# Four token mixers and a low-rank feed-forward network on one NeuronCore: where the network's first rows and fixed weights are loaded

## What is computed

```
x = x + L1_attn(_layernorm(x))             # Mamba2 mixer, chunked scan
x = x + L1_xattn(_layernorm(x), ctx, ctx)  # 8-head attention on the context
x = x + L1_ffn(_layernorm(x))              # low-rank experts:
  probs = softmax(x @ Wr + br); w, idx = top_k(probs, 2)
  h = x @ W1 + b1;  t1 = x @ A1 (8 experts, rank 16)
  a_e = gelu(h + 2 * t1_e @ B1_e)          # the two chosen experts
  mix = sum_e w_e * a_e;  t2_e = (w_e * a_e) @ A2_e
  out = mix @ W2 + sum(w) * b2 + 2 * sum_e t2_e @ B2_e
```

## Time and profile before

| | us |
|---|---|
| median of 3 runs | 3318.68 |
| lowest and highest run | 3313.62, 3318.94 |
| the profiled execution | 3309.98 |
| its span in the trace | 3308.3 |
| mean granted TensorE clock | 0.964 of full |
| TensorE, VectorE, ScalarE, POOL busy | 92%, 71%, 48%, 24% |

### The profile page before, as it was taken

One profiled execution on the slowest core, in us unless ns is written; L12 is line 12 of the kernel. 1 busy time (PEld: TensorE's weight loads), 2 busy tenths in 40 slices (PEclk: granted clock), 3 DMA queues, 4 the chain that ended last, 5 costly groups with the idle time before them and its releaser, 6 DMA issues. The chain is left out here.

```text
span 3308.3 us, 61051 instructions
## 1 busy us (share of the span) xinstructions
PE 3039.4 (92%) x22689; PEld 2437.3 (74%) x22689; DVE 2338.8 (71%) x4405; ACT 1597.3 (48%) x3656; POOL 803.8 (24%) x968
## 2 busy tenths in 40 slices
PE   7999999997998799999999859898999979999999
PEld 5666666664887688888888746666667668888888
DVE  5666666664765588888888666778786777777776
ACT  3333333342221455555555426566565756555555
POOL 1221122121454111111111153241423012222222
PEclk9999999998999899999999979899999989999999
DMA  6324233221121577777777621212110032222222
GB/s 261 128 71 175 108 128 110 108 102 39 29 57 34 198 239 238 247 250 243 243 243 240 236 82 65 71 39 72 58 59 20 8 126 89 74 74 77 74 74 71
DMA packets 144825, 401.85 MB, mean 121 GB/s; under 512 B 39056, under 2 KB 47760, under 8 KB 131680
## 3 DMA queue, kind: packets, MB, share of 16 engines
q1 hardware_dynamic: 106176, 323.30, 28.5%
q0 software_dynamic: 18976, 50.45, 5.2%
q10 hardware_dynamic: 19456, 25.18, 2.2%
HBM read 344.09 MB, written 54.76 MB: 121 GB/s over the span
## 5 line engine op out<-in xcount | busy, mean ns | idle before, releaser
L1465 POOL DMA_INDIRECT xg<-normed_rows,idx x128 | 124.8, 975 | 668.4 <-PE psum L1547 591.9
L2661 POOL TENSOR_TENSOR mixf<-act 128x256 f32<-128x256 f32 x128 | 143.5, 1121 | 470.5 <-DVE act L2942 470.5
L174 POOL TENSOR_SCALAR ve<-mv 128x1 f32<-128x1 f32 x112 | 36.7, 328 | 842.3 <-DVE mv L774 590.5
L1562 PE MATMUL psum<-xT_hi,wgu_hi 128*128 128x192 f32 (+1 forms) x1536 | 228.5, 271 | 4.2 <-ACT aT_lo L1529 4.2
L1562 PE MATMUL psum<-xT_lo,wgu_hi 128*128 128x192 f32 (+1 forms) x1536 | 223.3, 268 | 0.0
L1562 PE MATMUL psum<-xT_hi,wgu_lo 128*128 128x192 f32 (+1 forms) x1536 | 222.6, 267 | 0.0
L1601 DVE TENSOR_TENSOR wgu_lo<-wgu,wgu_hi 128x1408 fp32r<-128x1408 f32 x128 | 202.6, 1623 | 22.0 <-ACT wgu_hi L1489 22.0
L1562 PEld LDWEIGHTS psum<-xT_hi,wgu_hi 128*128 128x128 f32 (+1 forms) x1536 | 190.6, 182 | 28.8 <-ACT wgu_hi L1489 21.2
L1502 ACT ACTIVATE eth<-psum 128x192 f32<-128x192 f32 (+1 forms) x192 | 63.2, 329 | 298.1 <-PE psum L1562 295.2
L2019 ACT ACTIVATE scratch<-psum,smin 128x512 f32<-128x512 f32 x256 | 173.7, 686 | 58.3 <-DVE smin L2411 55.3
L2411 DVE TENSOR_REDUCE smin<-psum 128x2 f32<-128x1024 f32 x128 | 155.5, 1218 | 64.7 <-PE psum L2173 40.8
(11 more groups left out here) (436 smaller groups left out, 8592.9 us busy)
## 6 DMA issues: line engine op xcount, KB each, us to landing
wgu<-in_w_gu_dram SPq DMA_DIRECT2D x64, 1408.0 KB, 6.0
w_slot<-w_split SPq DMA_DIRECT2D x21, 2048.0 KB
wd<-in_w_d_dram SPq DMA_DIRECT2D x64, 512.0 KB, 8.7
w_raw<-in_w_dram SPq DMA_DIRECT2D x128, 256.0 KB, 2.6
expert_out<-yo ACTq DMA_DIRECT2D x64, 256.0 KB, 5.2
w_slot<-w_split SPq DMA_DIRECT2D x28, 512.0 KB
wd<-in_w_d_dram SPq DMA_DIRECT2D x64, 192.0 KB, 9.0
w_split<-w_slot SPq DMA_DIRECT2D x4, 2048.0 KB
```

The lines of the kernel that those rows point to most:

```text
L1465: pool.indirect_dma_start(out=xg[b][0:w, t, :], out_offset=None, in_=rows, in_offset=bass.IndirectOffsetOnAxis(ap=idx[b][0:w, t:t + 1], ax ...
L1562: ins = pe.matmul(bank(2 + m)[0:w, gu * CAP:(gu + 1) * CAP], wgu2[b][wp][:, gu, kc, m0:m0 + w], xT2[b][xp][:, kc, :], start=(i == 0 and kc ...
L2661: pool.tensor_tensor(mixf[:, g % LAG, :], act2[:, g % LAG, 0, :], act2[:, g % LAG, 1, :], ALU.add).then_inc(sy["f_mix"], 1)
```

## The change

In the last pair of `mixers`, SyncE issues three loads ahead of the load of the last context: the rows of sequence 0 from `mixed` into `xn[0]`, the first 1024 columns of `w_fixed` into `xn[1]`, and the last 32 (the router's) into a new small tile `router_raw`. They wait for the residuals of the sequences before and for the store of sequence 0. VectorE does the statistics of these rows in steps 12 and 13 of the last score loop and the norm in steps 18 and 19, in place, and POOL the reciprocal root. `xn[0]`, `xn[1]` and `router_raw` live on into `lora_ffn`, where the first two are `xin` and `xo`. There SyncE begins with the expanding pieces, then the small constants, and waits for the stores of `mixed` after these; at the end of `mixers` it waits for the two new loads alone. ScalarE and VectorE split the fixed weights in two instructions each, for 1024 and 32 columns.

```diff
@@ mixers, SyncE, in `for p in range(npair)`
+                if p + 1 == npair:
+                    sp.wait_ge(sy["resid_ready"], NT * first)
+                    sp.wait_ge(sy["mixed_out0"], 16)
+                    sp.dma_start(xn[0][:], dr["mixed"][0]).then_inc(sy["f_x_in"], 16)
+                    sp.dma_start(xn[1][:].rearrange("p t d -> p (t d)"), dr["w_fixed"][:, 0:NT * D]
+                                 ).then_inc(sy["f_fixed_in"], 16)
+                    sp.dma_start(router_raw[:], dr["w_fixed"][:, NT * D:NT * D + KC * LE]
+                                 ).then_inc(sy["f_fixed_in"], 16)
                 sp.wait_ge(sy["cx_lo_ready"], first + 1)
                 load_cx(second)
...
-            for b in range(2):
-                sp.wait_ge(sy[f"mixed_out{b}"], 16 * npair)
+            sp.wait_ge(sy["f_x_in"], 16)
+            sp.wait_ge(sy["f_fixed_in"], 32)
@@ mixers, POOL, end of a pair
+                else:
+                    norm(0, 2 * nseq)
@@ mixers, VectorE
+            def next_apply(j):
+                dve.wait_ge(sy["rstd_ready"], NT * 2 * nseq + j + 1)
+                dve.tensor_scalar(xn[0][:, j, :], xn[0][:, j, :], mv[0][:, j, 0:1], rstd[0][:, j:j + 1],
+                                  ALU.subtract, ALU.mult).then_inc(sy["normed_ready"], 1)
...
                     if i in (PAIRS + 3, HP + 3):
                         attended(first + i // PAIRS - 1, 1)
+                    if not more and i == 12:
+                        dve.wait_ge(sy["f_x_in"], 16)
+                    if not more and i in (12, 13):
+                        stats(0, i - 12, xn[0])
+                    if not more and i in (18, 19):
+                        next_apply(i - 18)
@@ lora_ffn, tiles and SyncE
-        xin, xo = sb("xin", [P, NT, D]), sb("xo", [P, NT, D])
+        xin, xo = rows
...
-        fixed_raw = act2[:].rearrange("p l k t -> p (l k t)")[:, 0:2 * D + KC * LE]
+        fixed_raw = [(slice(0, NT * D), xo[:].rearrange("p t d -> p (t d)")),
+                     (slice(NT * D, NT * D + KC * LE), router_raw[:])]
...
-            load_x(0)
-            for dst, src in ((fixed_raw, "w_fixed"), (br[:], "br_col"), (bias1[:], "bias1"),
-                             (bias2_bc[:], "bias2_bc")):
-                sp.dma_start(dst, dr[src]).then_inc(sy["f_fixed_in"], 16)
             for f in range(RAW):
                 load_up(f)
+            for dst, src in ((br[:], "br_col"), (bias1[:], "bias1"), (bias2_bc[:], "bias2_bc")):
+                sp.dma_start(dst, dr[src]).then_inc(sy["f_fixed_in"], 16)
+            for b in range(2):
+                sp.wait_ge(sy[f"mixed_out{b}"], 16 * nseq // 2)
...
+                        else:
+                            sp.wait_ge(sy["f_fixed_lo"], 1)
                         sp.dma_start(xo[:], dr["mixed"][s]).then_inc(sy["f_xo_in"], 16)
@@ lora_ffn, POOL, ScalarE, VectorE
-            rstd_pool(pool, sy, norms, mv, ve, rstd, const["minus_half"])
...
-            act.wait_ge(sy["f_fixed_in"], 16 * 4)
-            act.activation(fixed2[0][:], fixed_raw, ACT.Copy).then_inc(sy["f_fixed_hi"], 1)
+            act.wait_ge(sy["f_fixed_in"], 16 * 2)
+            for cols, raw in fixed_raw:
+                ins = act.activation(fixed2[0][:, cols], raw, ACT.Copy)
+            ins.then_inc(sy["f_fixed_hi"], 1)
...
+            act.wait_ge(sy["f_fixed_in"], 16 * 5)
             logits_copy(0)
...
-            stats(0)
-            layernorm_apply(dve, sy, norms, xin, xin, mv, rstd)
             dve.wait_ge(sy["f_fixed_hi"], 1)
-            dve.tensor_tensor(fixed2[1][:], fixed_raw, fixed2[0][:].bitcast(F32), ALU.subtract
-                              ).then_inc(sy["f_fixed_lo"], 1)
+            for cols, raw in fixed_raw:
+                ins = dve.tensor_tensor(fixed2[1][:, cols], raw, fixed2[0][:, cols].bitcast(F32), ALU.subtract)
+            ins.then_inc(sy["f_fixed_lo"], 1)
```

More of the change, by code:

```diff
@@ L1671, with mixer_weights @@
 SCALING = 2.0
-def mixer_weights(nc, ctx, dr):
+def mixer_weights(nc, ctx, dr, rows):
     shapes = {"w_in": [P, KC, D + XBC + MH], "small": [P, 64], "w_mo": [P, KC, D]}
@@ L1683, in mixer_weights, with mixers @@
     for s in range(4):
-        tiles[f"xn{s}"] = ctx.enter_context(nc.sbuf_tensor(f"xn3{s}", [P, NT, D], F32))
+        tiles[f"xn{s}"] = (rows[s] if s < len(rows) else
+                           ctx.enter_context(nc.sbuf_tensor(f"xn3{s}", [P, NT, D], F32)))
         loads.append((tiles[f"xn{s}"][:], dr["mid"][s]))
     return tiles, loads
-def mixers(nc, sy, const, dr, tiles, nseq=NSEQ):
+def mixers(nc, sy, const, dr, tiles, router_raw, nseq=NSEQ):
     with ExitStack() as ctx:
@@ L2533, with lora_ffn @@
 UPW = D + 2 * P
-def lora_ffn(nc, sy, const, dr, norms, nseq=NSEQ):
+def lora_ffn(nc, sy, const, dr, rows, router_raw, norms, nseq=NSEQ):
     with ExitStack() as ctx:
@@ L3076, in program @@
         dr["mixed"] = nc.dram_tensor("mixed", [NSEQ, P, NT, D], F32).ap()
[L3077 to L3080, removed]
+        with ExitStack() as carried:
+            rows = [carried.enter_context(nc.sbuf_tensor(f"xn3{b}", [P, NT, D], F32)) for b in range(2)]
+            router_raw = carried.enter_context(nc.sbuf_tensor("router_raw", [P, KC * LE], F32))
+            with ExitStack() as held:
+                tiles, loads = mixer_weights(nc, held, dr, rows)
+                if 2 in phases:
+                    phase2(nc, sy, const, dr, loads)
+                if 3 in phases:
+                    mixers(nc, sy, const, dr, tiles, router_raw, nseq)
             if 3 in phases:
-                mixers(nc, sy, const, dr, tiles, nseq)
-        if 3 in phases:
-            lora_ffn(nc, sy, const, dr, 2 * nseq, nseq)
+                lora_ffn(nc, sy, const, dr, rows, router_raw, 2 * nseq, nseq)
 def cols_layout(w):
```

## The result

| | before | after |
|---|---|---|
| median of 7 runs, us | 3318.68 | 3306.13 |
| lowest and highest | 3313.62, 3322.54 | 3303.8, 3311.08 |
| profiled execution, span | 3309.98, 3308.3 | 3304.07, 3302.3 |
| ratio after to before | | 0.9971, interval 0.9962 to 0.9980 |

The changed kernel is faster, by 6.6 to 12.6 us at this interval. The medians lie 12.5 us apart, the two profiled executions 6.0, and the forecast was 7.1. On another chip the same two kernels gave 0.9981 (0.9972 to 0.9990), 6.5 us between the medians. Both intervals hold the 6.7 us that the traces show at the place of the change.

The account below looks back on a forecast made before the run. At the boundary no engine was the bound, but a chain of single steps without work beside it. Boundary 8.0, less 1.3 in the last pair, plus 0.4 from the clock: 7.1 us less, 3311.6 us, range 3305 to 3317.

Parts of the forecast that it names:

- The boundary: Last store to router's start: wait, load and norm go, weights' split becomes late; 8.0 us gained, bounds 7.5 and 8.6.
- The last pair: Score loop: VectorE's pieces free in iterations 12 and 18, 0.82 and 0.5 at 13 and 19; +1.3 us, bounds 0 and 2.7.
- The weights' order: Start of the network's block: expanded weights first on SyncE, landing by 2664.1 and 2664.5 while the router runs; cost 0.
- The clock: Router: TensorE's clock mostly fallen at its start, back within its end; 0.4 of 2.4 us gained, bounds 0 and 2.4.
- Rival B: Clock stays at full level over the boundary, router done 2.4 us earlier; 9.1 us less, 3309.6; chance 0.17.
- Rival C: Clock comes back later behind the boundary, 6.6 us more at half level, 3.3 lost; 3.4 less, 3315.3; chance 0.20.
- Rival D: TensorE starves of instructions in the last pair or behind the boundary, 7 us stall; 2.6 slower, 3321.3; chance 0.08.
- A: The forecast itself for the whole kernel: 7.1 us less, own range 5.5 to 8.5 less, 3310 to 3313; chance 0.55.
- The median: Whole kernel: the 7.1 us gain taken off the earlier runs' median of 3318.68, giving 3311.6 us.

Follow-up runs that it names:

- wait_only: Kernel before the change, with only the wait for the last stores moved behind the network block's first loads; ratio 0.9999 (0.9990 to 1.0008), won 2.1 us.
- rows_only: Changed kernel, but the fixed weights are loaded at the start of the network's block, only the rows early; ratio 0.9993 (0.9984 to 1.0002), won 2.4 us.
- keep_wait: Changed kernel, but the mixers' block still ends only when the last stores have landed; ratio 0.9987 (0.9977 to 0.9997), won 5.0 us.
- weights_only: Changed kernel, but the first rows are loaded and normed in the network's block, only the weights early; ratio 1.0000 (0.9990 to 1.0009), won 1.8 us.
- idle_steps: Changed kernel with both statistics in step 12 and the norms in steps 22 and 24 of the score loop; ratio 0.9977 (0.9967 to 0.9987), won 8.0 us.
- after_again: The changed kernel, unaltered, measured once more against the kernel before on another chip; ratio 0.9981 (0.9972 to 0.9990), won 6.7 us.
- warm: Changed kernel plus 16 idle TensorE products at the mixers' end and 16 between first transposes and router; ratio 0.9978 (0.9969 to 0.9987), won 6.7 us.
- warm_short: Changed kernel plus 9 idle TensorE products at the mixers' end and 11 between first transposes and router; ratio 0.9965 (0.9951 to 0.9978), won 8.4 us.
- best: idle_steps plus fixed-weight columns 512 to 1023 split after the first expanding pieces, and 9 and 7 idle products; median 3235.32 against 3247.48, ratio 0.9956.

## Why the prediction was right

**The boundary.** 4.72 us from store to router forecast, 4.73 measured, but two of its steps were off by 0.4 us each and cancelled, which was luck. The block starts 0.83 us after the store's issue and not 0.43. With no wait between, it is 0.72 (wait_only), with one 0.77 (rows_only), with two 0.83; what the 0.72 consist of the traces do not show. The 0.07 that I had added for the step between blocks is what is left behind a landing that ends last, and the equal starts of two engines say nothing of its length. Against that, the splits and lower halves took 3.74 together (1.19, 1.32, 1.21 and the hand-overs), 0.4 less than the 4.10 forecast. The 1.44 that I had read for the two lower halves held the second one's wait for half-speed transposes. That the weights' split would be late next was right; keep_wait, rows_only and weights_only show each part of it.

**The last pair.** 1.3 forecast, 1.32 in the loop (57.75 to 59.07), with the cost at steps 13 and 19 alone. idle_steps shows it by moving them. The loads cost nothing there: from the store ahead of them to the loop it was 77.7 us before (2493.9 to 2571.6, mean clock 0.96) and 76.1 after (0.98). The 1.6 us between these are not the change's: wait_only, which has none of the loads, took 76.1 too (2428.2 to 2504.3), and after_again, which has them all, 77.7.

**The weights' order** on SyncE: the first expanding piece was awaited by ScalarE at 2664.83, 1.24 us, off the path, since the router needs neither.

**The clock.** I had put 0.4 us on the router's tail; it took 5.2, as before, so about 0.1 was had, and at the first gelu nothing of it is left (16.64 and 16.63). This is the 0.4 us by which the sum of 7.1 is above the 6.7 of the traces. The clock fell once more: a mean of 0.81 over 4.70 us is 1.8 us at the 1.2 GHz level, so it fell near 2663.5, after gaps of 2.44 and then about 1 us more. Rival B is refuted as to what the change does: the clock fell although no gap was longer than 2.8 us, and in idle_steps it fell at about 2590.9, within the first gap of 2.44. The Trainium skill (TensorE: Matmul & The Clock Gate, HAM oscillation), on whose rule B stood, warns only of idle gaps longer than a limit. The traces do not agree with it here. warm and warm_short show B's price to be nearly right for the router, 2.2 us instead of 2.4, of which 2.1 and 1.7 reach the first gelu.

Rival C's condition came in good part, and its price did not. Before, the second stretch at half level ended 2.1 us behind the first gelu (2690.2 and 2688.08). In the changed kernel it ran from 2677.1 to 2687.4, so it ended 5.4 us behind the first gelu (2681.95), 3.3 us later. By the reckoning of C half of that, 1.7 us, would be lost, but the rest grew by only 0.13. In best the half level lasted until 6 us behind the first gelu, and the rest is 620.32. The first unit is not bound by TensorE. Its chain in the changed kernel goes through the other engines:

```profile
2683.18 0.96 DVE w_up_lo L2964
...
2684.83 1.12 POOL mixf L2685
```

Rival D did not show: TensorE ran 72.5 of 76.1 us at the beginning of the last pair. The stall from which D was reckoned stands in each of the first three loops, with waits of 8.05, 7.38 and 6.66 us ahead of one minima, and likewise in the other five traces with spans of 3299 us or more. In the six with spans of 3232 to 3241 us there is none, and in the last pair none in any trace. So this stall goes with the chip and with the pairs that have gathers, not with the change; what causes it the traces do not show.

**The median.** 3311.6 forecast, 3306.13 measured. The 5.5 us too much are not a step of the sum: the traces give 6.7 against 7.1. They are the draw of the two sets of runs, as the 6.5 us on the other chip show: luck, which put the median outside A's own 3310 to 3313 and only 1.1 us above the lower end of the range. The reason that the runs of one kernel differ by 9 us here, and by 16 among 31 runs of the kernel before beside warm, was only placed (ahead of the last loop), not explained.

## What to carry to other kernels

Two loads that lie side by side ahead of a block's first work are worth moving only together: one alone gave nothing and the other 1.8 us of the 6.3. Work that was moved into the running loop was free in a step where its engine waited, and cost nearly its full length where the next instruction had no idle time before it, so read the idle time in brackets step by step before choosing the step. After such a move look at what ran beside the removed steps: it is the next chain, and here a split not yet needed and a lowered clock were worth another 3.2 us (11.1 in best against 8.0 in idle_steps). A lowered clock costs only where TensorE leads the chain: in the router, and not in the first unit.

## What the runs showed of the hardware

- The first 512 KB load of a block, issued 0.72 us after a 512 KB store on the same queue, was used 4.19 us after its issue (wait_only); issued when that store had landed, 3.5 (before).
- TensorE's clock went to its lower level at the boundary although the engine's two idle gaps were 2.44 and 2.80 us with 1.06 us of work between. Unused products in these gaps kept it at the full level and saved 2.2 us in the router. With 9 and 11 of them the router started only 0.06 us later, and 1.7 us were won in all.
- A float32 product of 128 columns took 0.23 to 0.24 us at the full clock and stands in the trace as two matmuls.
